# A four-layer sequence model on one core: new places for all parts of both phases' engine orders, and one more wait in `pe_f_a`

## The reference, cut to what matters

```python
x = x + L0_attn(layernorm(x))   # "s": gated scan (a selective state space layer)
x = x + L0_ffn(layernorm(x))    # "g": eight experts, gate keeps at most two above 1/8
x = x + L1_attn(layernorm(x))   # "t": 16 heads of 8 + 4 rotary features, causal softmax
x = x + L1_ffn(layernorm(x))    # "f": silu(w1 x) * (w2 x), two 512x512 layers with gelu, w3
...
h = a_t * h + bx_t[..., None]   # the scan of "s": 256 channels x 16 states, 512 steps
y = c_t * jnp.sum(h, axis=-1)
```

## Time and profile before

| | |
|---|---|
| time, median of 3 runs | 1684.76 us (1684.6 to 1685.74) |
| span of the profiled execution, first to last instruction | 1683.4 us |
| mean granted TensorE clock | 0.953 of full speed |
| first and last end of layer "s" (DVE L663 starts) | 92.3 and 1191.8 us |
| last end of layer "t" (DVE L1158 starts) | 1321.3 us |
| first product of phase two (PE L1472 starts) | 1323.9 us |
| last store issued | 1676.9 us |

### The profile page before, as it was taken

The page is one execution under the profiler, slowest core; times in us unless marked ns, Lnnn a source line. Parts: engine busy times, 40 slices in busy tenths (PEclk is TensorE's granted clock), DMA queues, the critical chain, the costliest instruction groups (busy, mean ns, idle before and its releaser), DMA issues.

```text
span 1683.4 us, 24214 instructions
## 1 busy us (share of the span) xinstructions
PE 1510.7 (90%) x7815; PEld 799.2 (47%) x7815; DVE 1401.6 (83%) x2550; ACT 1267.5 (75%) x2176; POOL 1251.9 (74%) x1211
## 2 busy tenths in 40 slices
PE   5256799999999999999999999998999899999997
PEld 2123244443444444444444344433444578888886
DVE  4899899999999999999999998998541477987773
ACT  5776798988989898898989898896646555555552
POOL 4988798988989898898989898898332345555553
PEclk8576999999999999999999999999999899999999
DMA  4000000000000000000000000000200000000000
GB/s 150 1 0 1 19 1 20 13 7 20 1 20 2 19 11 10 19 1 20 1 19 5 16 20 1 19 1 20 79 11 20 1 1 13 14 13 14 13 13 27
DMA packets 14686, 27.58 MB, mean 16 GB/s; under 512 B 3981, under 2 KB 4566, under 8 KB 14042
## 3 DMA queue, kind: packets, MB, share of 16 engines
q1 hardware_dynamic: 14554, 25.98, 5.5%
HBM read 9.20 MB, written 4.19 MB: 8 GB/s over the span
## 4 chain that ended last, share of the span: by engine, by line
PE 50%; POOL 20%; DVE 15%; ACT 7%; issue 7%; DMA 1%; SPq 0%; POOLq 0%; ACTq 0%; DVEq 0%
PE bank L1041 9%; POOL sum_fast L641 8%; PE bank L1523 7%; PE bank L1499 6%; DVE state_fast L623 5%; PE bank L695 5%; PE bank L1108 4%; PE bank L494 3%; POOL prob_fast L1091 3%; ACT prob_fast L1057 2%; PE bank L728 2%; POOL g_prod_fast L871 2%; PE bank L1543 2%; ACT state_fast L608 2%; PE bank L897 2%
## 5 line engine op out<-in xcount | busy, mean ns | idle before, releaser
L641 POOL TENSOR_TENSOR sum_fast<-sum_fast,state_fast 128x512 f32<-128x512 f32 x448 | 584.4, 1304 | 69.5 <-DVE state_fast L623 31.9
L623 DVE TENSOR_TENSOR_SCAN state_fast<-state_fast,bank 128x512 f32<-128x512 f32 x512 | 596.0, 1199 | 6.9 <-ACT state_fast L608 6.8
L1057 ACT ACTIVATE prob_fast<-bank 128x1024 f32<-128x1024 f32 x320 | 325.8, 1020 | 120.1 <-PE bank L1041 112.3
L1041 PE MATMUL bank<-stacks_fast 64*128 64x512 f32 (+3 forms) x2048 | 369.7, 470 | 18.3 <-ACT prob_fast L1057 11.8
L608 ACT ACTIVATE state_fast<-chan_all_kept,neg_a_fast 128x512 f32<-128x512 f32 x512 | 347.6, 714 | 10.2 <-POOL sum_fast L641 5.2
L1041 PEld LDWEIGHTS bank<-stacks_fast 64*128 64x128 f32 x2048 | 173.2, 188 | 241.2 <-ACT prob_fast L1057 106.9
L1091 POOL TENSOR_SCALAR_AFFINE_SELECT prob_fast<-prob_fast 128x512 f32<-128x512 f32 x256 | 167.7, 669 | 123.0 <-ACT prob_fast L1057 122.9
L1108 PE MATMUL bank<-prob_fast,v_ext_fast 128*32 128x512 f32 (+3 forms) x2048 | 182.4, 459 | 41.9 <-POOL prob_fast L1091 40.7
L1712 POOL TENSOR_TENSOR cell_a_fast<-th_fast,cell_a_fast 128x512 fp32r<-128x512 f32 x64 | 90.3, 1411 | 143.1 <-ACT cell_a_fast L1584 143.0
L728 PE MATMUL bank<-we_t_fast,xnt_g_fast 128*128 128x512 f32 x256 | 139.9, 640 | 2.8 <-DVE own_fast L858 1.0
L695 PE MATMUL bank<-resid_m_fast,xnt_g_fast 128*128 128x512 f32 x256 | 128.9, 616 | 10.2 <-DVE gate_fast L778 7.8
(11 more groups left out here) (214 smaller groups left out, 2664.5 us busy)
## 6 DMA issues: line engine op xcount, KB each, us to landing
stacks_fast<-parts_fast SPq DMA_DIRECT2D x128, 64.0 KB
stacks_fast<-rest_fast SPq DMA_DIRECT2D x128, 32.0 KB
out_x<-f_out_fast SPq DMA_DIRECT2D x16, 256.0 KB, 2.0
x_res_kept<-in_x SPq DMA_DIRECT2D x1, 2048.0 KB, 13.9
chan_all_kept<-in_h_t SPq DMA_DIRECT2D x2, 1024.0 KB, 7.9
x_res_kept<-in_x SPq DMA_DIRECT2D x1, 1024.0 KB, 9.5
chan_all_kept<-in_w_t SPq DMA_DIRECT2D x3, 256.0 KB, 2.9
x_res_kept<-in_x SPq DMA_DIRECT2D x2, 256.0 KB, 3.3
```

What stands on the lines that cost most here:

```text
L623: dve.tensor_tensor_scan(h[:], h[:], self.banks[0][:], 0.0, ALU.mult, ALU.add).then_inc(self.v_scan.sem)
L641: pool.tensor_tensor(total[:], total[:], h[:], ALU.add).then_inc(self.p_sum.sem)
L1041: ins = pe.matmul(self.scores(b, step)[:, c:c + SEQ - P * kt], rows[:, 1, h // 2, P * kt:P * kt + P], rows[:, 0, h // 2, P * kt:SEQ], star ...
L1057: act.activation(self.probs[u % 2][:, i * 1024:(i + 1) * 1024], self.scores(b, 5 * g + n)[:], ACT.Exp, scale=SCALE).then_inc(self.a_prob.sem)
```

## The change

Every number of `PERIOD`, `F_PERIOD`, `TIMES` and `EDGES` is replaced. Strands, parts and instructions are the same, and each engine has as many as before. `EDGES` now shifts more strands (the setup ones, `act_f_first`, `dve_f_first`, `pe_f_first`, `sp_loads` and others), so that the first three and last three sequences differ more from the middle. One wait is changed: `pe_f_a(0)` now waits for the split of sequence 1 too, since the new order leaves that split, which reads bank 1, to the end of phase one.

```diff
-PERIOD, F_PERIOD = 72141, 24942
+PERIOD, F_PERIOD = 72295, 27783
...
-    "pool_masks": [187767, 192304, 196813, 205195, 212359, 214741, 221805, 230054, 235427, 242160, 249726, 250305],
...
+    "pool_masks": [180206, 196271, 199060, 207561, 211284, 218458, 220794, 225948, 228687, 240553, 242015, 244353],
...
-    "pe_f_first": [114892, 144949],
...
+    "pe_f_first": [61523, 230423],
...
-    "dve_f_first": [98073, 113813, 116748, 123982, 232653],
...
+    "dve_f_first": [136320, 163139, 188710, 284366, 374766],
...
             if mt == 0:
-                pe.wait_ge(split.sem, split.at(b))
+                pe.wait_ge(split.sem, split.at(max(b, 1)))
```

More of the change, by code:

```diff
@@ new lines @@
+    "act_f_rstd": [346727],
+    "act_f_turned": [68249],
+    "act_g_gate": [109523, 110020, 116121, 119017],
+    "act_g_rstd": [74245],
+    "act_g_setup": [54419, 58737, 63269, 76694, 89847],
+    "act_g_squares": [89117, 89388, 94019, 95146, 99100, 100750, 106517, 106517],
+    "act_g_turned": [86161],
+    "act_g_xn": [79620],
+    "act_inputs": [-19842, 19077],
+    "act_nums": [200848, 216071, 238898, 256394, 264359],
+    "act_s_head": [-29367, -24527, -22120, -20290, -7969, -1816, 15451],
@@ new lines @@
+    "act_s_rstd": [-157721],
+    "act_s_turned": [-63335],
+    "act_s_xn": [-130336],
+    "act_scores": [182821, 186476, 190212, 193742, 199743, 200402, 206119, 207287, 207287, 209079, 214292, 215474,
+        222599, 227480, 233258, 239127, 242668, 244740, 249779, 253335],
+    "act_setup": [-277303, -95799],
+    "act_t_proj": [169320, 174138, 180781],
+    "act_t_rstd": [141094],
+    "act_t_setup": [54663, 112688, 113537],
+    "act_t_turned": [144954],
+    "act_t_xn": [141494],
+    "dve_bound": [238353],
@@ new lines @@
+    "dve_setup": [-176319, -88866, -81621, -68020, -68020, -56735, -35148],
+    "dve_t_norm": [137443],
+    "dve_t_out": [269640],
+    "dve_t_proj": [156533, 165521, 182960, 189496],
+    "dve_values": [206005, 227241, 243558, 260524],
+    "pe_bound": [180401],
+    "pe_f_a": [95341, 98344, 106145, 114147],
+    "pe_f_first": [61523, 230423],
+    "pe_f_flags": [497905],
+    "pe_f_h1": [124071, 128648, 135023, 145371],
+    "pe_f_h2": [164287, 165987, 178317, 186304],
+    "pe_f_out": [217153, 232291],
@@ new lines @@
+    "pe_setup": [-706078],
+    "pe_t_out": [265226, 269429],
+    "pe_t_proj": [153693, 161083, 168304, 171882, 179466, 186381],
+    "pe_t_setup": [9611, 72293, 118638],
+    "pe_t_turn": [149137],
+    "pe_values": [195331, 198177, 199785, 204885, 212445, 214544, 220056, 226209, 231893, 236385, 236385, 242272,
+        250852, 253874, 254707, 260194],
+    "pool_f_a": [121846, 126143, 132270, 133093],
+    "pool_f_h1": [152688, 174846],
+    "pool_f_h2": [192297, 212508],
+    "pool_g_sums": [126155, 126270, 129569, 134577],
@@ L148 @@
+    "sp_loads": [-705943],
+    "sp_rows": [307777, 314748, 317000, 328924, 345837, 362438],
+    "sp_weights": [236048],
 }
 EDGES = {
[L150 to L153, removed]
```

189 lines of the change are left out of this document (76 added, 113 removed).

## The result

The kernel after takes 1627.49 us (median of 4 runs, 1626.18 to 1629.97), the kernel before in the same comparison 1685.25: a ratio of 0.9649, 95% interval 0.9632 to 0.9665. The change is faster by 3.5%, 57.8 us. The forecast was 1660 us, 25 gained, and its range ended at 1642. The sign was right, the size was not.

What follows compares the result with a forecast made beforehand. No single engine bounded the kernel; the four queues' waits for each other set the middle's period. 1684.8 - 22 (middle) - 3 (ramp) + 0.2 (added wait) = 1660 us; own range 1650 to 1672, 8 in 10 range 1642 to 1688.

Steps and rivals of the forecast that it cites:

- The stall and the clock: Middle, PE: the 2.24 us wait at values.13 and the clock fall behind it go, 0 to 3.8 us a period.
- The loop's legs: Middle: the four legs through POOL, ACT, PE and DVE change to sum to 70.8 us, so this loop no longer decides.
- The loop as I drew it: Middle of before: a once-a-period chain through POOL, ACT, PE and DVE whose legs sum to 74.7 us.
- What comes next: Middle, POOL: new waits at masks.0, masks.10, masks.11 and masks.5 on 66.72 us of work make a 72.5 us period.
- The gate's chain: Middle, DVE: small g_gate.2 operations could lose 0.96 us or more a period; counted as nothing, 12 us if on the path.
- Rival 3: Middle: DVE becomes the bound, the period falls to 71.0 us, 41 us gained, 1641 us; chance 0.12.
- The ramp: Start of phase one: POOL has more sums done early, 3 us gained, bounds -5.3 to +2.5.
- The drain: End of phase one: PE busy 56.46 of 58.00 us, so next to nothing to gain.
- The added wait: Start of phase two: PE waits for the split of sequence 1, costing 0.1 to 0.2 us, about 1.9 if uncovered.
- the tail: Before the last f_out: a block fills PE's 2.14 us wait for POOL; nothing either way, within 0.5 us.
- phase two: Body of phase two: PE stays full, 322.76 of 324.00 us busy; nothing counted for the new order.
- The signs named in advance: Profile after: periods 72 to 73 us, no values.13 stall, clock 1.00, POOL waits 3 to 5, phase two's first product 2.5 to 2.8.

Runs made afterwards that it cites:

- e3: Kernel before with only masks.10 and masks.11 moved two sums and one sum earlier on POOL: 1657.89 us, ratio 0.983.
- e7: Kernel after with masks.10 and masks.11 put back behind sums.21 on POOL: 1672.74 us, ratio 0.990.
- e4: Kernel before with masks.10 and masks.11 early and masks.0 ahead of sums.23 on POOL: 1677.87 us, ratio 0.995.
- e8: Kernel after with masks.0 put back behind sums.24 on POOL: 1641.78 us, ratio 0.973.
- e14: Kernel after with POOL's old order, except masks.10, masks.11 and masks.0 early: 1666.07 us, ratio 0.989.
- e15: Kernel after run once more, unchanged: 1628.98 us, ratio 0.966 to before.
- e1: Kernel after with the old orders of phase two, the added wait kept: 1631.63 us, ratio 0.967.
- e12: Kernel after with sequence 1's turn, copy and split moved ahead of t_out15 on PE, ACT and DVE: 1630.70 us.
- e2: Kernel before with the new orders of phase two and the added wait: 1686.37 us, ratio 1.000.
- e6: Kernel after with POOL's old order in phase one: 1674.36 us, ratio 0.991.
- e5: Kernel before with POOL's whole new order in phase one: 1725.58 us, ratio 1.021.
- e11: Kernel after with decays.30 and decays.31 ahead of scores.1 on ACT, as before: 1644.75 us, ratio 0.974.
- e13: Kernel after with POOL's old order, except masks.10 and masks.11 early: 1681.20 us, ratio 0.997.

## Why the forecast had the sign and not the size

- **The stall and the clock.** Right in sign. The wait at `values.13` is gone and the clock is 1.00 in the middle. e3 puts it at 2.4 us a period in the old orders, within the 0 to 3.8 given. In the new ones it is 3.7 (e7).
- **The loop's legs.** The leg sum of 70.8 was meant to say that the loop no longer decides; the period is 70.43, so this estimate was the nearest of all, though nothing shows that it is more than luck. The loop as I drew it is not shown to be what held before: e3 went below its 73.1 us by moving two masks that stand on none of its legs.
- **"What comes next" is the step that failed.** It added to POOL's 66.72 us of work waits of 3.6 at `masks.0`, 1.3 at `masks.10` and `.11`, and 0.9 for `masks.5`: 72.5 us. That is 5.8 us of waits on top of work. In after POOL waits 2.15 us, at `masks.0` alone. The wait itself was no fancy: e4 has 3.88 us. But even there only 1.45 us a period are lost by it, since it takes the place of the 2.5 us that POOL waited for DVE in e3. (The 1.10 us that I started from are those of two of the nine middle periods of before; the other seven have 2.7.) What was wrong is that I took the wait from the old orders of PE and ACT and added it to work, as if POOL were the bound. In the new orders it stands in the place of a wait for DVE that POOL would have anyway, 3.13 us in e8, and taking it away makes the kernel 1.15 us a period slower. The waits put at `masks.10`, `.11` and `masks.5` did not appear at all. The sum was not one that gives a period, either: POOL's short idle stretches, 3.2 us a period in before, are missing from it, and beside a wait that is counted in full they would have made it 75.7. The period is 2.1 us shorter than this term made it, 27 of the 33 us missed (1660 against 1627); the next point is a part of these 27.
- **The gate's chain.** I counted nothing. L833 is 164 ns at most where L826 had 1124 in the median, and L821 fell to 184 from 614 (L814 before). Its share is bounded by e8: 0.87 us of DVE's work and 1.15 of the period. So DVE's "floor" of 70.25 was none: the same instructions take 68.9 in after, where POOL stands still beside most of the chain. The rule of the Trainium skill (SBUF — State Buffer, Who interferes with whom) that I set beside the row would have given 12 us, and e8 x 13 gives 15: the row and the rule deserved a place in the sum. That the two agree is partly luck. The operation of the row is as short without this change (161 ns in the median in e3 and in e8, where `masks.0` stands behind the sums); what `masks.0` releases is L821. The hold falls on whichever small operation a sum happens to meet. e14 bounds the claim: 68.0 us of DVE work, and yet 72.6 a period.
- **Rival 3, DVE as the bound,** had 0.12 and was the closest of the cases: 71.0 forecast, 70.43 measured, DVE 98% busy, though PE is as full. Its two conditions (waits under each other, the gate's chain released) are what after shows beside e8.
- **The ramp.** 3 us forecast, bounds -5.3 to +2.5. At the end of "s" of sequence 0 the profile is 4.7 us ahead, inside the bounds; 9.6 us at sequence 2, of which a part is the chance of this pair of profiles. Four profiles have the new orders there (after, e15, e1, e12) and end "s" of sequence 2 at 221.5 us in the mean; two have the old ones (227.26 in before, 223.99 in e2), 225.6 in the mean. So some 4 us are the ramp's, near the 3 forecast, and one profile alone does not show them. A kernel with the ramp alone was not tried.
- **The drain** was put at next to nothing by a row that covers 58 of its 129.5 us; in the whole of it PE was busy 122.76 us, so 6.7 were free. It gave 3.5 us, and with e2's 130.4 us against 125.4 to 126.3 in the four profiles of the new orders it is no chance. Which of the new places did it was not examined.
- **The added wait, the tail, phase two.** 0.1 to 0.2 forecast, 0.16 measured; nothing and nothing, as forecast (e1, e2).
- **The signs named in advance.** The stall, the clock and the first product of phase two (2.71 us after L1165) came as said. The ends of layer "s" are 70.4 us apart and not 72 to 73, and POOL waits 2.15 us for ACT and not 3 to 5.

What stays open: which of the new places of PE, DVE and ACT fit which of POOL's. By their ratios to before, POOL's new order is worth 44 us with the new three (e6 to after) and costs 36 with the old ones (before to e5), but the new orders of PE, DVE and ACT were only tried together.

## What to carry to other kernels

Where four queues are each some 90% busy or more, the price of a move is not a property of the move: the same two masks gave 29 us or none, the same wait cost 1.45 us a period and saved 1.15, by what the other engines did. A new wait may be added to an engine's work only if that engine has no other pause that the wait would fill; look for what it would wait for next. And the busy time of an engine that contends with another is no floor: read the same small operation's fastest and median duration first.

## What was not expected of the hardware

The ramp's length varies with the same orders of phase one. The end of "s" of sequence 2 stands at 217.70 and 220.86 us in two profiles of after, at 223.43 in e1 and 223.94 in e12, which differ only behind it. In the windows from 180 to 200 us the two long ones have a granted clock of 0.83, the short ones 1.00, with PE 15.8 to 16.6 of 20 us busy (after, then e1):

```profile
180.00:200.00 20.00, 16.55 (x86) 6.64 (x86) 18.90 (x34) 18.04 (x31) 14.92 (x18) 1.00 0.10 19
```

```profile
180.00:200.00 20.00, 16.29 (x66) 7.42 (x68) 18.49 (x31) 14.37 (x25) 11.77 (x11) 0.83 0.11 24
```

That is 3 to 6 us, as much as the forecast gave the whole ramp. The kernel before does the same: 227.26 us, and 223.99 in e2, which has its orders of phase one. These two both have 0.83 in that window, so the clock there does not tell a short ramp from a long one. Whether it is the cause or follows the late work is not settled.

In the middle the clock held at 1.00 through pauses of up to 1.6 us on PE in all nine periods of e14 and in eight of e6. It fell behind most pauses of 2.2 us and more in before and in e7, but not behind each: the period of 73.09 us has the first pause of the earlier trace rows, 2.24 us, and a clock of 1.00. And in e11 and e13, whose longest pauses are 1.3 and 1.6 us, the mean is 0.99: it fell in three and in four of the nine periods there. The length of one pause does not decide it.
